# Sums of squares from two matmuls of split operands, for three chunks of four

## The reference

```python
q, k = rope(xn @ Wq.T), rope(xn @ Wk.T)          # 32 heads, 8 key/value heads, head size 128
v = xn @ Wv.T
scores = einsum(qc, kc)                          # per chunk of 128 tokens
y_intra = einsum(scores * decay, xc)
y_inter = einsum(qc * exp(G), prev)              # prev: running state of earlier chunks
y = y_intra + y_inter
rms = sqrt(mean(square(y), axis=-1) + RMS_EPS)   # over the 128 values of a head
y = y / rms * gnorm_w
y = y * (gate * sigmoid(gate))
return y @ Wo.T
```

## Time and profile before

| | us |
|---|---|
| median of 3 runs | 2372.81 (2370.6 to 2373.22) |
| the profiled execution: its time | 2377.89 |
| its span, first to last instruction | 2375.8 |

### The profile page before, as it was taken

One profiled execution on the slowest core, in us unless ns is written; L12 is line 12 of the kernel. 1 busy time (PEld: TensorE's weight loads), 2 busy tenths in 40 slices (PEclk: granted clock), 3 DMA queues, 4 the chain that ended last, 5 costly groups with the idle time before them and its releaser, 6 DMA issues.

```text
span 2375.8 us, 35103 instructions
## 1 busy us (share of the span) xinstructions
PE 2154.5 (91%) x9788; PEld 1704.4 (72%) x9788; DVE 1890.2 (80%) x3422; ACT 1381.8 (58%) x2668; POOL 1189.4 (50%) x888
## 2 busy tenths in 40 slices
PE   6699999999999999996999999999999999778775
PEld 6577777777777777764777777777777777566653
DVE  3488888888888888866888888888888887577765
ACT  2366666666666666633666666666666766444430
POOL 6245454545444444533454545545454554666646
PEclk9999999999999999997999999999999999888886
DMA  4312121212121111133121212122121211577767
GB/s 172 126 39 62 35 68 38 62 35 62 35 65 43 56 49 53 50 106 120 36 63 38 62 44 56 50 51 58 42 62 44 65 36 45 177 240 233 234 202 230
DMA packets 155565, 198.60 MB, mean 84 GB/s; under 512 B 13831, under 2 KB 90215, under 8 KB 155518
## 3 DMA queue, kind: packets, MB, share of 16 engines
q1 hardware_dynamic: 139742, 163.86, 23.9%
q0 software_dynamic: 7424, 21.00, 2.7%
q10 hardware_dynamic: 8352, 13.17, 1.6%
HBM read 169.65 MB, written 28.33 MB: 83 GB/s over the span
## 4 chain that ended last, share of the span: by engine, by line
issue 43%; POOL 27%; DVE 10%; PE 8%; DMA 6%; ACT 3%; SPq 2%; POOLq 1%; ACTq 0%; DVEq 0%
POOL gm L687 5%; POOL zl L425 5%; DMA gate<-in_wm 4%; POOL ql L694 3%; POOL wgl L646 3%; POOL wol L646 3%; POOL wql L646 2%; DVE wol L1784 2%; POOL vl L708 2%; POOL kl L694 1%; POOL wkvl L646 1%; DVE vwl L1556 1%; POOL slot_tokens L737 1%; DMA gbc<-decay_exponents 1%; DVE yb L1500 1%
## 5 line engine op out<-in xcount | busy, mean ns | idle before, releaser
L425 POOL TENSOR_TENSOR zl<-yb,zh 128x512 fp32r<-128x512 f32 x130 | 172.7, 1328 | 351.1 <-ACT zh L881 350.9
L1084 PE MATMUL OU<-woh,zh 128*128 128x512 f32 x520 | 243.5, 468 | 16.0 <-POOL wol L646 11.7
L1535 DVE TENSOR_TENSOR t<-PJ,cosb 128x512 f32<-128x512 f32 x160 | 110.2, 689 | 176.1 <-PE PJ L1086 132.9
L1084 PE MATMUL PJ<-xnh,wqh 128*128 128x512 f32 x544 | 226.5, 416 | 21.5 <-DVE t L1537 20.4
L1086 PE MATMUL PJ<-xnh,wql 128*128 128x512 f32 x544 | 216.2, 397 | 0.0
L1085 PE MATMUL PJ<-xnl,wqh 128*128 128x512 f32 x544 | 216.1, 397 | 0.0
L899 ACT ACTIVATE qh<-t 128x512 fp32r<-128x512 f32 x128 | 81.0, 633 | 221.5 <-DVE t L1540 221.5
L1084 PE MATMUL PJ<-xnh,wgh 128*128 128x512 f32 x512 | 204.7, 400 | 0.0
L1086 PE MATMUL OU<-woh,zl 128*128 128x512 f32 x520 | 204.4, 393 | 0.0
L1085 PE MATMUL OU<-wol,zh 128*128 128x512 f32 x520 | 204.2, 393 | 0.0
L1086 PE MATMUL PJ<-xnh,wgl 128*128 128x512 f32 x512 | 200.4, 391 | 0.0
(11 more groups left out here) (479 smaller groups left out, 6710.9 us busy)
## 6 DMA issues: line engine op xcount, KB each, us to landing
gbc<-decay_exponents SPq DMA_DIRECT2D x128, 256.0 KB, 4.8
gate<-in_wm SPq DMA_DIRECT2D x48, 512.0 KB, 4.3
stage<-in_wq SPq DMA_DIRECT2D x72, 256.0 KB, 3.9
stage<-in_wg SPq DMA_DIRECT2D x64, 256.0 KB, 2.7
stage<-in_wo SPq DMA_DIRECT2D x64, 256.0 KB, 2.7
gbc<-in_wm SPq DMA_DIRECT2D x48, 256.0 KB, 3.0
expert_rows<-rs ACTq DMA_DIRECT2D x48, 256.0 KB, 3.1
stage<-in_wkv SPq DMA_DIRECT2D x34, 256.0 KB, 2.6
```

The source lines that it names most:

```text
L425: nc.gpsimd.tensor_tensor(lo[:], yb[:, c, :], hi[:].bitcast(F32), ALU.subtract).then_inc(S["zlo"], 1)
L1084: nc.tensor.matmul(out_, a_hi, b_hi, start=first, stop=False)
```

## The change

For chunks 0 to 2 the float32 matmul with `y2` becomes two matmuls of type float32r. ACT squares `yb[:, c]` into `rs[:, c]` (free until the result of that chunk is copied there), and copies it to the high part `y2h`; POOL subtracts to the low part `y2l`; PE multiplies both by the ones of type float32r into TR. Chunk 3 keeps the float32 matmul and reads `rs[:, 3]`. `t1` and `y2` become float32 views of the memory of `y2l` and `y2h`. The wait for the last sum is moved behind the low part: `squares(c)` waits for `sqlo`. DVE's first rotary step of a step waits for the third sum of the step before. Two semaphores of the routing are folded into others.

```diff
+                        def sq_lo(c):
+                            at.wait("sqhi", c + 1)
+                            if c:
+                                at.wait("ssq", c)
+                            else:
+                                at.wait("rope", 5)
+                            g.tensor_tensor(y2l[:], rs[:, c, :], plain(y2h[:]), ALU.subtract).then_inc(S["sqlo"], 1)
+
...
                         for c in range(NCH - 1):
+                            if c:
+                                sq_lo(c - 1)
                             z_lo(pool, at, c + 1)
...
+                        sq_lo(2)
...
                             at.wait("y", c + 1)
-                            a.activation(y2[:], yb[:, c, :], ACT.Square).then_inc(S["ysq"], 1)
+                            at.wait("z", c + 1)
+                            a.activation(rs[:, c, :], yb[:, c, :], ACT.Square).then_inc(S["ysq"], 1)
+                            if c < 3:
+                                at.wait("ysq", c + 1)
+                                if c == 0:
+                                    at.wait("tr", 1)
+                                a.activation(y2h[:], rs[:, c, :], ACT.Copy).then_inc(S["sqhi"], 1)
...
                         def squares(c):
 
-                            at.wait("ysq", c + 1)
                             if c:
                                 at.wait("ssqc", c)
-                            nc.tensor.matmul(TR[:], ones[:], y2[:], start=True, stop=True).then_inc(S["ssq"], 1)
+                            if c < 3:
+                                at.wait("sqlo", c + 1)
+                                nc.tensor.matmul(TR[:], onesr[:], y2h[:], start=True, stop=False)
+                                nc.tensor.matmul(TR[:], onesr[:], y2l[:], start=False, stop=True).then_inc(S["ssq"], 1)
+                            else:
+                                at.wait("ysq", 4)
+                                nc.tensor.matmul(TR[:], ones[:], rs[:, 3, :], start=True, stop=True).then_inc(
+                                    S["ssq"], 1)
...
                             if i == 0:
                                 at.before("ropelo", 4)
+                                at.before("ssq", 3)
...
-            act.wait_ge(rsoft, 1)
-            a.activation(sm, sm, ACT.Exp).then_inc(rexp, 1)
+            act.wait_ge(to_act, 4)
+            a.activation(sm, sm, ACT.Exp).then_inc(to_dve, 1)
```

More of the change, by code:

```diff
@@ L104, in build @@
         vf = sb("vf", [P, 512])
-        t1 = sb("t1", [P, 512])
+        y2l = sb("y2l", [P, 512], F32R)
         t2 = sb("t2", [P, 2, 512])
-        y2 = sb("y2", [P, 512])
+        y2h = sb("y2h", [P, 512], F32R)
         gate = sb("gate", [P, HG, 512])
@@ L148, in plain @@
             return t.bitcast(F32)
+        t1, y2 = as_f32("y2l"), as_f32("y2h")
         khf, klf, vhf, vlf, zhf, qhf, qlf = [as_f32(name) for name in ("kh", "kl", "vh", "vl", "zh", "qh", "ql")]
@@ L262, in build @@
             proj=10, tr=2, score=4, cstate=3, yinter=3, yintra=4, ssq=4, oproj=4,
-            vraw=1, ropehi=5, vhi=1, knhi=1, dec=4, expg=3, vwhi=3, whi=4, sthi=3, tanh=4, ysq=4, ssqc=4,
+            vraw=1, ropehi=5, vhi=1, knhi=1, dec=4, expg=3, vwhi=3, whi=4, sthi=3, tanh=4, ysq=4, sqhi=3, ssqc=4,
             rsln=1, rms=1, zhi=4,
             coef=1, roperd=5, rope=5, q3lo=1, knlo=1, wsc=4, wlo=4, vwlo=3, stt=3, stlo=3, yt=3, y=4, gated=4, u=4, z=4, accd=4,
-            ropelo=4, vlo=1, gmask=4, zlo=4,
+            ropelo=4, vlo=1, gmask=4, zlo=4, sqlo=3,
         )
@@ L323, in build @@
         cleared = sem("cleared")
-        rsoft = sem("rsoft")
-        rexp = sem("rexp")
         rk_made = sem("rk_made")
@@ L1683, in route_scores @@
                 link(v.tensor_reduce(mx1[:, :, 0], rlg, AX.X, ALU.max))
-                v.tensor_tensor(sm, rlg, mx1.broadcast_to([P, NTA, E]), ALU.subtract).then_inc(rsoft, 1)
+                v.tensor_tensor(sm, rlg, mx1.broadcast_to([P, NTA, E]), ALU.subtract).then_inc(to_act, 1)
             def route_groups():
-                dve.wait_ge(rexp, 1)
+                dve.wait_ge(to_dve, 5)
                 link(v.tensor_reduce(sum1[:, :, 0], sm, AX.X, ALU.add))
```

## The result

| | before | after |
|---|---|---|
| median | 2373.01 (2370.6 to 2374.91) | 2490.44 (2488.02 to 2492.12) |
| the profiled execution: its time | 2377.89 | 2492.12 |
| its span | 2375.8 | 2490.3 |
| mean granted TensorE clock | 0.965 | 0.945 |

The ratio is 1.0494, with a 95% interval of 1.0478 to 1.0511: the change costs 117 us. The forecast of 2431 had the sign right and half of the size, and the time lies outside its range. A step of the attention, from the start of `squares(0)` to the start of the next one, was 56.5 us with b = 0 and 56.7 us with b = 1. After, in the first half of the attention, four of the eight steps with b = 0 are 58.2 us and the others 59.5 to 60.9, and most of those with b = 1 are 61.25. In the second half most are 59.35 (b = 0) and 60.3 (b = 1).

A forecast was written before the change was run, and what follows sets the result against it. DVE and ACT's round trip was taken to pace the loop up to intra(3), PE what follows; steps 1.46 (b = 0) and 2.18 us (b = 1) longer, times 16, give 58 us, 2372.8 to 2431; range 2366 to 2455.

The forecast's parts named there:

- what the prediction worked out: Attention steps at unchanged PE speed: 1.46 us longer with b = 0, 2.18 with b = 1, over 16 of each, 58 us.
- The bound, and the slack at intra(3): Delays ahead of intra(3) count only as far as they move the last wfl, less 0.07 us slack; behind it PE decides.
- DVE held by POOL: In rounds 1 to 3 late_z or wfl stands beside sq_lo, ending 0.55 us behind POOL; intra(3) +1.86 (b = 0), +2.58 (b = 1).
- ACT's copy: y2h between square and wfh in each round: moves wfh by 0.65 us where ACT is later, by less where DVE is.
- PE's saving: Two float32r matmuls for one float32 square save 0.40 us; only that of squares(2), behind intra(3), counts in full.
- the thing to look for: Sign in the changed kernel's timelines: PE idle 2 us or so ahead of intra(3), with wfl as its releaser.
- the rest: Delays of z_lo, new waits and routing semaphores, together 0; at most one 1.3 us subtraction a step, put into the range.

The follow-up runs named there:

- filled: Changed kernel plus useless matmuls on PE just ahead of intra(3) in round 3, 8 with b = 0 and 12 with b = 1; 2451.38 us, ratio 1.0334.
- slots later: Filled kernel with POOL's four indirect DMAs in the second half's b = 0 steps moved from round 0 to round 1; 2439.51 us, ratio 1.026.
- moved chunk 1: Changed kernel with only chunk 1 split, ACT's copy put behind wfh of the next round and sq_lo ahead of z_lo(3); 2363.86 us, ratio 0.9949.
- saving undone: Changed kernel with copy and subtraction kept, but the float32 matmul of rs in all four chunks; 2494.85 us, ratio 1.0509.
- The copy alone: Changed kernel without POOL's subtraction; PE takes the float32 square of rs but waits for ACT's copy; 2402.17 us, ratio 1.0125.
- half of the fill: Filled kernel with half as many useless matmuls, 4 with b = 0 and 6 with b = 1; 2452.53 us, ratio 1.0313.
- only chunk 2 split: Changed kernel with the split in chunk 2 alone, chunks 0, 1 and 3 by the float32 matmul of rs; 2414.34 us, ratio 1.0154.
- low part left out, with the copy: Changed kernel without POOL's subtraction and the second matmul, ACT's square and copy kept; 2369.11 us, ratio 0.9974.
- filled with b = 1 alone: Filled kernel with only the 12 useless matmuls of b = 1, none with b = 0; 2469.91 us, ratio 1.0388.

## Why the prediction was wrong, point by point

The experiments part the 117 us, by the ratios and a time before of 2373:

| | ratio | us |
|---|---|---|
| the change | 1.0494 | 117 |
| less the lower clock (filled) | 1.0334 | 38 |
| less POOL's queue in the second half (slots later) | 1.0260 | 18 |
| left: what the prediction worked out | | 62 |

Each of the two differences is uncertain by some 6 us. The steps are the sharper measure: the queue is 1.05 us in 8 steps, 8 us, and what the prediction worked out is 4.05 us in 16 pairs, 65 us. With the clock's 38 that makes 111 of the 117 us; the rest is within the uncertainty of the ratios.

**The bound, and the slack at intra(3): right.** PE idles 2.10 and 3.13 us ahead of `intra(3)` and `wfl` is its releaser, as said.

**DVE held by POOL: right, to a tenth or two.** With b = 0, y(0) to y(1) is 511.70 - 501.34 = 10.36 us against 9.64 of the earlier trace rows, +0.72 (worked: +0.7); y(2) comes another 0.98 later (519.19 - 511.70 against 838.19 - 831.68; worked: 1.6 - 0.7 = 0.9); `intra(3)` starts 21.82 us behind y(0) instead of 19.86, +1.96 (worked: +1.86). With b = 1, from the end of `wfl(1)` to that of `wfl(2)` it is 573.99 - 564.30 = 9.69 against 8.69 of the earlier trace rows, +1.00 (worked: 2.16 - 0.98 = 1.18), and on to that of `wfl(3)` 7.90 against 7.40, +0.50 (worked: 0.49). The hand-over of 0.55 behind POOL's end came out the same in all 87 hits. The Trainium skill, "SBUF — State Buffer", section "Who interferes with whom", calls the shared port pair an exclusive lock, and gives it, for DVE's 2-port modes, to the first one for its whole instruction; by the trace the held DVE instruction ends 0.55 behind POOL's, less than the 0.68 that it takes alone. The same section of the Trainium skill says that the order of issue decides who blocks; the moved chunk 1 agrees: there POOL was the one held, 1.68 for 1.30.

**ACT's copy: right in the sum.** Alone it is dearer than the 0.6 us a step expected of that experiment (0.7 and 0.8); 0.14 of this stands behind `intra(3)`, see the next point.

**PE's saving: 0.40 worked, 0.25 seen.** From `intra(3)` to `squares(3)` it is 2.98 us in the kernel before and 2.73 in the filled kernel. With the saving undone it is 3.12, so the saving itself is there, 0.39; but 0.14 is lost to something that all the changed kernels share (0.11 to 0.14 in each) and for which the prediction had nothing. It stands in two places. First the last start before `squares(3)` and that of `squares(3)`, before and in the filled kernel:

```profile
844.65 0.39 PE L1086 MATMUL OU<-woh,zl 128*128 128x512 f32 x1
844.88 1.12 PE L1211 MATMUL TR<-y,ones 128*128 128x512 f32 x2
...
518.55 0.40 PE L1102 MATMUL OU<-woh,zl 128*128 128x512 f32 x1
518.86 1.10 PE L1232 MATMUL TR<-rs,ones 128*128 128x512 f32 x2
```

0.31 for 0.23. The other 0.06 lies between the first two matmuls of `intra(3)`, 516.45 - 516.11 = 0.34 against 0.28 before. It makes 4 to 5 us in 32 steps, about the difference between the worked 58 us and what is left. Its cause is not shown; no run varied it alone. And in time the saving brought the changed kernel nothing: undoing it moves it by less than the uncertainty.

**The sum of these: 62 to 65 us measured, 58 predicted.** The steps of the filled kernel are 4.05 us longer in a pair, the prediction had 3.64.

**First step that failed: there was no term for the clock.** I had worked out the idle time, had even named it as the thing to look for, and took the rest of the step at its old speed. The forecast should have asked what PE does *behind* an idle time of 2 or 3 us. The trace of before has no idle time of this length in the attention's steps, but it has them where a half of the attention ends, and there the price could be read:

```profile
1032.42 0.54 PE L1084 MATMUL OU<-woh,zh 128*128 128x512 f32 x1 [2.98 <-POOL zl L425]
1032.76 0.63 PE L1085 MATMUL OU<-wol,zh 128*128 128x512 f32 x1
1033.18 0.63 PE L1086 MATMUL OU<-woh,zl 128*128 128x512 f32 x1
```

Behind 2.98 us of idle time the starts are 0.43 apart, down to 1035.74. An idle time of 2.51 us that ends at 1023.71 has full speed behind it, one of 1.96 us that ends at 2011.72 has the lower clock again. So the trace said that it can happen, if not how often. And a bound was at hand: `intra(3)` and the eight matmuls behind it up to `squares(3)` are 11 starts of 0.231, and at half of the clock each costs that much again, 2.5 us. Measured with b = 1: 61.25 against 59.03, 2.2 us, in the first half; in most steps of the second, 60.3 against 58.9, 1.4 us.

**Second: "the rest" at 0.** I wrote that POOL is free before the high parts are made, from a step of the first half. In the second half POOL's queue holds the slot DMAs in just the round in which `sq_lo(0)` is due. The prediction's upper bound for this place, one subtraction of 1.3 us in a step, was of the right order: 59.35 - 58.3 = 1.05 us in each step with b = 0 of that half. It was put into the range, and not into the sum, because no step of the second half had been read.

**What stays open.** The copy alone costs 28 to 30 us where 19 were expected of that experiment; the steps show some 25 of them (0.57 and 0.68 ahead of `intra(3)`, 0.14 behind it), and what makes the 0.14 is open. Whether a POOL instruction that reads nothing in SBUF would hold `wfl` as well; it wasn't tried. And what, beside the length of an idle time, decides whether the clock falls (counts below).

## What to carry to other kernels

Where a change makes the busiest engine wait, read what comes behind the wait too: here a third of the loss was TensorE at half of its clock behind 2 to 3 us of idle time. A split that takes 0.4 us from PE costs a copy and a subtraction elsewhere, and on POOL that subtraction held the DVE instructions with two SBUF inputs (`late_z`, `wfl`, `vwl`) that came while it ran; whether it pays depends on which of the two starts first, so it belongs behind the DVE instruction of the round trip, and not in a row with other POOL work. Read one step of each kind, and of each phase of the kernel in which a queue holds other work.

## What the runs showed of the hardware

How often a lower granted clock stood within some 6 us of the end of PE's idle time ahead of `intra(3)`:

| kernel, b | idle us | times of |
|---|---|---|
| half of the fill, 0 and 1 | 1.1, 1.7 | 0 of 32 |
| only chunk 2 split, 0 and 1 | 1.16 | 2 of 32 |
| low part left out, with the copy, 1 | 1.8 to 2.3 | 5 of 16 |
| saving undone, 0 | 1.67 | 10 of 16 |
| saving undone, 1 | 2.4 to 2.7 | 11 of 16 |
| changed kernel, 0 | 2.1 | 6 of 16 |
| filled with b = 1 alone, 0 | 2.15 | 12 of 16 |
| changed kernel, 1 | 3.1 | 16 of 16 |

So it becomes likelier with longer idle time, but the length alone does not part the cases; even 1.16 us was followed by it twice. Nor is it the same in every place of a step: ahead of its `scores` PE idles up to 1.59 us in 15 steps with b = 0, in the kernel before and in the changed one alike, and no lower clock followed any of them, while behind the 1.67 us ahead of `intra(3)` it came in 10 of 16. I had expected neither the fall behind so short a stop, nor that less work on PE could cost time through it.

The second finding is how unequal the two orders are. The POOL subtraction of the moved chunk 1, which starts second, is lengthened from 1.30 to 1.68 us by a DVE subtraction of 0.68; a DVE instruction that starts second ends 0.55 behind POOL, and `late_z` then takes 1.78 for 0.74. The loser loses 0.4 in one order and 1.0 in the other.
